# Two scan stages: the product with B made by TensorE for some state pairs, more C products on GpSimd

## The reference

```python
Bm, Cm = jnp.split(xs @ xp_w, 2, axis=-1)
dt = jax.nn.softplus(Bm @ dt_w + dt_b)
def step(hst, inp):
    xt, dtt, Bt, Ct = inp
    dA = jnp.exp(dtt[..., None] * A)
    hst = hst * dA + dtt[..., None] * Bt[:, None, :] * xt[..., None]
    yt = jnp.sum(hst * Ct[:, None, :], -1)
    return (hst, yt)
...
y = (y + D_skip * xs) * jax.nn.silu(gate)
```

## Time and profile before

| | us |
|---|---|
| median of 3 runs (5192.56 to 5204.24) | 5202.94 |
| the profiled execution, its time | 5190.3 |
| its span | 5188.7 |
| TensorE busy | 4065.8 (78%) |
| VectorE busy | 3570.5 (69%) |
| ScalarE busy | 2530.8 (49%) |
| GpSimd busy | 2856.4 (55%) |

### The profile page before, as it was taken

One profiled execution on the slowest core, in us unless ns is written; L12 is line 12 of the kernel. 1 busy time (PEld: TensorE's weight loads), 2 busy tenths in 40 slices (PEclk: granted clock), 3 DMA queues, 4 the chain that ended last, 5 costly groups with the idle time before them and its releaser, 6 DMA issues. The chain is left out here.

```text
span 5188.7 us, 47328 instructions
## 1 busy us (share of the span) xinstructions
PE 4065.8 (78%) x13734; PEld 1854.4 (36%) x13734; DVE 3570.5 (69%) x4968; ACT 2530.8 (49%) x3913; POOL 2856.4 (55%) x2181
## 2 busy tenths in 40 slices
PE   7999527982956988888887798997789777777776
PEld 2444203750423653333332444543333222222222
DVE  7998426121545759999998644444443699999999
ACT  5553311330445876666665244444346555555554
POOL 3776451027034439999996301113331489988997
PEclk8999759995977999999999899988889899999999
DMA  1100200211111115444443333321110343334443
GB/s 48 51 35 35 76 33 25 68 52 53 55 74 48 58 50 169 155 153 153 155 153 110 86 45 40 43 40 40 32 41 17 109 137 135 133 134 140 136 135 102
DMA packets 161701, 434.82 MB, mean 84 GB/s; under 512 B 28151, under 2 KB 51385, under 8 KB 160049
## 3 DMA queue, kind: packets, MB, share of 16 engines
...
## 5 line engine op out<-in xcount | busy, mean ns | idle before, releaser
L1680 ACT ACTIVATE mb_h<-m_dt,m_a_neg 128x512 f32<-128x512 f32 x1024 | 665.0, 681 | 725.8 <-DVE r L1835 332.9
L1539 PE MATMUL mb_y<-r,m_diag_y 128*128 128x512 f32 x1024 | 549.3, 671 | 273.0 <-POOL r L1760 164.6
L1826 DVE TENSOR_TENSOR_SCAN mb_h<-mb_h,m_u 128x1024 f32<-128x1024 f32 x320 | 733.9, 2294 | 10.8 <-DVE mb_h L1815 0.5
L1783 POOL TENSOR_TENSOR m_u<-m_bsb,m_xs 128x1024 f32<-128x1024 f32 x256 | 600.2, 2369 | 175.7 <-DMA m_bsb<-bc_rows 175.7
L1783 POOL TENSOR_TENSOR m_u<-m_bsb,m_dtx 128x1024 f32<-128x1024 f32 x256 | 596.0, 2359 | 50.9 <-DVE m_dtx L1867 28.2
L1539 PE MATMUL mb_y<-m_hc,w_common 128*128 128x512 f32 x1024 | 499.6, 628 | 149.5 <-DVE m_hc L1835 84.6
L1826 DVE TENSOR_TENSOR_SCAN m_hs<-mb_h,m_u 128x1024 f32<-128x1024 f32 x192 | 437.6, 2279 | 1.7 <-POOL m_u L1783 1.7
L1539 PEld LDWEIGHTS mb_y<-r,m_diag_y 128*128 128x128 f32 x1024 | 196.3, 207 | 621.0 <-POOL r L1760 245.3
L2309 DVE TENSOR_REDUCE at_mx<-at_ps_s 128x4 f32<-128x512 f32 (+1 forms) x256 | 243.2, 957 | 235.2 <-PE at_ps_s L2123 235.1
L1760 POOL TENSOR_TENSOR r<-m_hs,m_csb 128x1024 f32<-128x1024 f32 x128 | 308.2, 2408 | 118.0 <-DVE m_hs L1826 117.4
L1539 PEld LDWEIGHTS mb_y<-m_hc,w_common 128*128 128x128 f32 x1024 | 191.5, 197 | 449.2 <-issue 195.0
...
## 6 DMA issues: line engine op xcount, KB each, us to landing
m_bsb<-bc_rows SPq DMA_DIRECT2D x256, 512.0 KB, 4.9
m_csb<-bc_rows SPq DMA_DIRECT2D x256, 512.0 KB, 4.0
...
```

The costliest lines, as they stand in the source:

```text
L1539: mm = nc.tensor.matmul(ps_y[:, h], weight, hc[:, q % RING, s], start=False, stop=g == GROUPS - 1 and s == SG - 1)
L1680: ins = nc.scalar.activation(ps_h[:, q % 2, s], dt[:, i % 2, h], ACT.Exp, scale=a_neg[:, n:n + 1])
L1783: nc.gpsimd.tensor_tensor(u[:, q % RING], bsb[:, n % RING], dtx[:, i % 2, h].unsqueeze(1).broadcast_to([P, SG, TILE]), ALU.mult).then_inc( ...
L1826: V.tensor_tensor_scan(flat(to), flat(ps_h[:, q % 2]), flat(u[:, q % RING]), 0.0, ALU.mult, ALU.add).then_inc(h_ready, 1)
```

## The change

For some pairs (`by_pe`) the product with B is made by TensorE: pairs 4 to 7 of 8 in layer 2, all but pairs 0 and 4 in the last layer. A product u[d, t] = z[d, t] B[t] is a matmul of z, transposed to tokens by channels, with a diagonal matrix of B. Tokens are taken in four interleaved quarters k (t = 4r + k) and two rows j of 256, so a diagonal is 64 by 64.

- `turn_z` transposes z (dtx or x) of the next tile and `copy_z` (ScalarE) copies it to `zt`; `turn_b` and `copy_b` do so for B, into `bt`.
- `diagonals` (GpSimd) makes the diagonals of one pair into `dg` (2 slots) from a constant, `spots`, and `bt`.
- `make_u(q)` (TensorE) is 8 matmuls, 64 rows by 128 columns, rows 0 to 63 and 64 to 127 in turn, each into its own bank of `ps_h[:, q % 2]`. TensorE does it four units ahead in its order, before `sum_states(q - 4)`.
- For these units the decays go to SBUF, into the ring `u`, and the term lies in PSUM; the columns are ordered row, state, token, which `packed` and `spread` undo at the C product. Their B is not fetched, and `bsb` has 2 or 3 slots.
- C products: GpSimd takes all in the last layer and 9 of 16 in layer 2 (before 8 and 4), out of three `hs` slots.
- Silu, gate and project steps move by a unit or so, and take waits on `z_ready` and `z_in`.

The diff, cut to its core:

```diff
+    BR, HS = (3, 3) if l3 else (2, 3)
...
+        bsb = sb("bsb", [P, BR, SG, TILE])
...
+        hs = sb("hs", [P, HS, SG, TILE])
+        zt = sb("zt", [P, 2, 2, 4, P])
+        bt = sb("bt", [P, 2, 4, NSTATE])
+        dg = sb("dg", [P, 2, 4, SG, T // 4])
...
-        by_pool = [q % (2 if l3 else 4) == 0 for q in range(NU)]
+        by_pool = [True if l3 else q * 9 % 16 < 9 for q in range(NU)]
+        by_pe = [q % UNITS // 2 % 4 != 0 if l3 else q % UNITS // 2 >= 4 for q in range(NU)]
+        pe_units = [sum(by_pe[:q]) for q in range(NU + 1)]
+        fed_units = [q - pe_units[q] for q in range(NU + 1)]
+        z = xs if l3 else dtx
...
+        def slot_free(q, eng):
+
+            if q >= 2 and by_pool[q - 2]:
+                eng.wait_ge(h_ready, q - 1)
+            if q >= 2 and not by_pool[q - 2]:
+                eng.wait_ge(hc_ready, dve_units[q - 1])
...
                 elif a:
                     pe.wait_ge(sg_ready, 2 * a)
+                    pe.wait_ge(z_ready, 2 * a)
...
+                if h:
+                    pe.wait_ge(bt_ready, a + 1)
                 nc.tensor.matmul(ps_w[:, h], w["dt_w"][0:K, h * P:(h + 1) * P], low[0:K],
                                  start=True, stop=True).then_inc(dt_in, 1)
...
+            def turn_b(a):
+                pe.wait_ge(low_ready, a + 1)
+                rows_b = bcf[0:NSTATE].rearrange("p (r k) -> p k r", k=4)
+                for k in range(4):
+                    mm = nc.tensor.transpose(ps_w[:, 1, k * NSTATE:(k + 1) * NSTATE], rows_b[:, k],
+                                             w["eye"][0:NSTATE, 0:NSTATE])
+                mm.then_inc(bt_in, 1)
...
+                cols = z[:, a % 2, h].rearrange("p (r k) -> p k r", k=4)
+                for k in range(4):
+                    mm = nc.tensor.transpose(ps_w[:, bank, k * P:(k + 1) * P], cols[:, k], w["eye"])
+                mm.then_inc(z_in, 1)
+
+            def make_u(q):
+                i, g, h = place(q)
+                d = pe_units[q] // 2
+                pe.wait_ge(z_ready, 2 * i + 2)
+                pe.wait_ge(d_ready, d + 1)
+                slot_free(q, pe)
+                to = ps_h[:, q % 2].rearrange("p j (s r k) -> p j k s r", s=SG, k=4)
+                for k in range(4):
+                    for j in range(2):
+                        at = slice(j * 64, (j + 1) * 64)
+                        mm = nc.tensor.matmul(to[:, j, k], zt[at, i % 2, h, k], dg[at, d % 2, k], start=True, stop=True)
+                mm.then_inc(u_made, 1)
...
-                pe.wait_ge(dt_taken, 2 * min(i + 2, NT))
+                pe.wait_ge(dt_taken, 2 * min(i + 3, NT))
+                pe.wait_ge(z_ready, 2 * min(i + 2, NT))
...
+            turn_b(0)
             step_size(0, 0)
             step_size(0, 1)
+            turn_z(0, 0)
+            turn_z(0, 1)
+            for q in range(4):
+                if by_pe[q]:
+                    make_u(q)
...
-                    sum_states(i * UNITS + n)
+                    q = i * UNITS + n
+                    if q + 4 < NU and by_pe[q + 4]:
+                        make_u(q + 4)
+                    sum_states(q)
                     if n == (3 if l3 else 2) and more:
                         project(i + 1)
                     if n == (5 if l3 else 3) and more:
+                        turn_b(i + 1)
                         step_size(i + 1, 0)
                         step_size(i + 1, 1)
                     if n == (9 if l3 else 7) and i:
                         project_out(i - 1)
-                    if n == (11 if l3 else 10) and more:
+                    if n == 9 and l3 and more:
+                        turn_z(i + 1, 0)
+                    if n == 10 and l3 and more:
+                        gate(i + 1, 0)
+                        turn_z(i + 1, 1)
+                    if n == 12 and l3 and more:
+                        gate(i + 1, 1)
+                    if n == 10 and not l3 and more:
                         gate(i + 1, 0)
                         gate(i + 1, 1)
+                    if n == 14 and not l3 and more:
+                        turn_z(i + 1, 0)
+                        turn_z(i + 1, 1)
             project_out(NT - 1)
...
+            def copy_b(a):
+                act.wait_ge(bt_in, a + 1)
+                if a >= 2:
+                    act.wait_ge(d_ready, pe_units[(a - 1) * UNITS] // 2)
+                nc.scalar.copy(bt[:, a % 2].rearrange("p k n -> p (k n)"), ps_w[:, 1, 0:4 * NSTATE]).then_inc(bt_ready, 1)
+
+            def copy_z(a, h):
+                act.wait_ge(z_in, 2 * a + h + 1)
+                if a >= 2:
+                    act.wait_ge(u_made, pe_units[(a - 1) * UNITS])
+                nc.scalar.copy(zt[:, a % 2, h].rearrange("p k d -> p (k d)"), ps_w[:, 1 if l3 else h]).then_inc(z_ready, 1)
...
-                if n == (4 if l3 else 3):
+                if n == 4:
...
                 if n == (8 if l3 else 6):
+                    copy_b(a)
                     step_parts(a, 0)
+                if n in (11, 13) and l3:
+                    copy_z(a, n // 13)
                 if n == (8 if l3 else 7):
...
-                if n == 14 and a:
+                if n == (15 if l3 else 13) and a:
...
+                if by_pe[q]:
+                    if q >= RING:
+                        act.wait_ge(h_ready, q - RING + 1)
+                    to, step = packed(u[:, q % RING], q), dt[:, i % 2, h].rearrange("p (j t) -> p j t", j=2)
+                else:
+                    slot_free(q, act)
+                    to, step = ps_h[:, q % 2].unsqueeze(1), dt[:, i % 2, h].unsqueeze(1)
                 if q == 1:
                     act.wait_ge(sg_ready, 2)
                 for s in range(SG):
                     n = h * NSTATE + g * SG + s
-                    ins = nc.scalar.activation(ps_h[:, q % 2, s], dt[:, i % 2, h], ACT.Exp, scale=a_neg[:, n:n + 1])
+                    ins = nc.scalar.activation(to[:, :, s], step, ACT.Exp, scale=a_neg[:, n:n + 1])
                 ins.then_inc(da_ready, 1)
...
+                if not l3 and q >= UNITS and q % UNITS == 3:
+                    copy_z(q // UNITS, 0)
+                    copy_z(q // UNITS, 1)
...
+                    k = fed_units[2 * n] // 2
+                    if not by_pe[2 * n]:
+                        if k >= BR:
+                            sync.wait_ge(u_ready, (k - BR + 1) * 2)
+                        src = bc_d[i % 2, g * SG:(g + 1) * SG].rearrange("s t -> (s t)").unsqueeze(0).broadcast_to([P, SG * TILE])
+                        sync.dma_start(bsb[:, k % BR].rearrange("p s t -> p (s t)"), src).then_inc(b_in[k % BR], 16)
+                    if n >= RING:
                         free = (n - RING + 1) * 2
-                        if n >= RING and dst is bsb:
...
+                        if dve_units[free]:
                             sync.wait_ge(hc_ready, dve_units[free])
-                            if pool_units[free]:
-                                sync.wait_ge(hp_ready, pool_units[free])
-                        src = bc_d[i % 2, at:at + SG].rearrange("s t -> (s t)").unsqueeze(0).broadcast_to([P, SG * TILE])
-                        sync.dma_start(dst[:, s].rearrange("p s t -> p (s t)"), src).then_inc(done[s], 16)
+                        sync.wait_ge(hp_ready, pool_units[free])
...
+                nc.gpsimd.tensor_tensor(spread(hc[:, q % RING], q), packed(hs[:, k % HS], q), spread(csb[:, n % RING], q),
+                                        ALU.mult).then_inc(hp_ready, 1)
...
+                i, g, h = place(q)
+                d = pe_units[q] // 2
+                pool.wait_ge(bt_ready, i + 1)
+                if d >= 2:
+                    pool.wait_ge(u_made, 2 * (d - 1))
+                nc.gpsimd.tensor_tensor(dg[:, d % 2], w["spots"].unsqueeze(1).unsqueeze(1).broadcast_to([P, 4, SG, T // 4]),
+                                        bt[:, i % 2, :, g * SG:(g + 1) * SG].unsqueeze(3).broadcast_to([P, 4, SG, T // 4]),
+                                        ALU.mult).then_inc(d_ready, 1)
...
+                k = fed_units[q] // 2
+                if not by_pe[q]:
+                    pool.wait_ge(b_in[k % BR], (k // BR + 1) * 16)
+                    if q >= RING:
+                        pool.wait_ge(h_ready, q - RING + 1)
+                    nc.gpsimd.tensor_tensor(u[:, q % RING], bsb[:, k % BR],
+                                            dtx[:, i % 2, h].unsqueeze(1).broadcast_to([P, SG, TILE]), ALU.mult).then_inc(u_ready, 1)
+                if q + 4 < NU and by_pe[q + 4] and q % 2 == 0:
+                    diagonals(q + 4)
                 if q >= 3 and by_pool[q - 3]:
                     times_c(q - 3)
-                if q % UNITS == UNITS - 1 and i + 1 < NT:
...
+                if by_pe[q]:
+                    dve.wait_ge(u_made, pe_units[q + 1])
+                else:
+                    dve.wait_ge(u_ready, fed_units[q + 1])
...
```

(38 more changed lines are left out.)

56 lines of the change are left out of this document (37 added, 19 removed).

## The result

The changed kernel takes 5912.68 us (5899.93 to 5919.80), the kernel before 5197.75 us beside it: ratio 1.138, 95% interval 1.1342 to 1.1417. The forecast was 5690, the range 5420 to 5900. So the direction held, the size did not: 489 us of growth were predicted, 715 came.

What follows compares the result with a forecast made beforehand. VectorE was taken to bound both scan stages, GpSimd close behind. Inner tiles add 14 x (17.6 + 15.4) = 462 us; with first tiles, last tiles and lead-in 489; 5190 + 489 = 5679, forecast 5690, range 5420 to 5900.

Steps and rivals of the forecast that it cites:

- the loads: Scan stages: VectorE 59.3 and 48.2 us a tile; by loads alone a tile would be 60.6 and 53.3.
- rival 1: Both scan stages: loads decide, stalls overlap the work of others; 142 us saved, 5061; chance 0.10.
- make_u at 1.1: TensorE: 8 matmuls in overlapping row groups, 8 x 0.112 + 0.2 = 1.1 us each.
- The diagonals were booked at 1.28: GpSimd: 512-column diagonals take 1.28 us; short broadcast runs could make them up to 2.4.
- The places of the stalls: Inner tiles: VectorE waits at listed places, sum 26.3 us in the last layer and 22.0 in the second.
- The clock: TensorE, both stages: granted 0.97 and 0.94, so nearly all at 2.4 GHz; a lower clock kept for the upper end.
- the second layer's conv: Second layer: conv waits for z_ready, given by copy_z after decay(3), and delays decay(5); stall 3.6 us.
- the 0.6 us of copy_low: Last layer, after scan 5: make_u(7), sum(3), projections, copy_low and decay(7) hold up VectorE; stall 4.8 us.
- Edges: First tiles plus 10 (last layer) and 5 (second); last tiles plus 4 and 0; lead-in plus 4 each.
- (d) in the second layer: After C product 12: make_u(14), sum(10), gate, table loads, silus, decay(14) take 9.2 against 2.35; stall 6.9 us.
- The range: Whole kernel: 5420 with half of the stalls hidden, to 5900 with a slow make_u and a lower clock.
- rival 3: TensorE: make_u takes 2.0 us, giving 5790; at 3.9 TensorE is the bound and it passes 5900; chance 0.13.

Runs made afterwards that it cites:

- Experiment 6: The changed kernel, but TensorE makes no product with B (those stay on GpSimd) and the decays stay in PSUM: 5521.7 us, ratio 1.060.
- experiment 9: The kernel before, with zero-weight matmuls in TensorE's two longest idle stretches of a last-layer tile: 5199.2 us against 5195.4, ratio 1.0004.
- experiment 5: The changed kernel, with zero-weight matmuls only in TensorE's idle stretches, each group shorter than its stretch: 5751.3 us, ratio 1.105.

## Why the prediction came out short

Point by point, by its own steps:

- **What bounds it, and the loads**: right. In the kernel after VectorE is busy 927.5 us in the last stage, 58.0 a tile (booked 59.3), and 46.9 a tile in the second layer's (booked 48.2). Experiment 6 shows GpSimd's at 80.0 and 63.9 (booked 81.3 and 64.3, for that mix). That loads would not decide was right as well; rival 1 (5061) is out.
- **make_u at 1.1**: right. At the full rate the next instruction starts 1.09 us after it (4834.25 to 4835.34). The diagonals were booked at 1.28 and took 1.05; short runs did not lengthen them, they are faster.
- **The places of the stalls**: right, all ten. With TensorE at full rate their sum is 27.8 in the last layer (booked 26.3; the 0.5 and 0.3 of two small ones are in it) and 23.8 in the second (22.0).
- **The clock: this is the step that failed.** The prediction took the granted clock of the kernel before, 0.97 and 0.94, booked every make_u and every sum of its chains at 2.4 GHz, and kept a lower clock as a margin above, without a price. But in the kernel before TensorE is slow beside a busy VectorE, where it costs nothing (experiment 9); in the kernel after it is slow at the head of the chains. Its slow stretches follow from the stalls that the prediction had listed itself: in the last layer each of its three long waits for a scan (3.18, 5.58 and 6.32 us) is followed by a make_u of 2.08 instead of 1.16 and, in the rows above, a sum of 3.15 to 3.70 instead of 1.98. In the last layer the filled stretches took 8.5 us off each tile (95.6 to 87.1), in the second 3.3 (75.1 to 71.8): 14 x 11.8 = 165 us, where the kernel gained 161 as a whole.
- **The account of the difference.** Predicted 489, measured 715, so 226 are missing. (It is 223 against 5690, since the forecast stood on 5203 for the kernel before and was rounded.) Over the 14 periods between the first and the fifteenth gate product, the second layer grew by 284 us (booked 216) and the last by 386 (booked 246): 208 of the 226. The filled idle stretches give back 46 and 120 of them (experiment 5): 166 are the clock. Some 25 are the second layer's conv, in part at half rate (1.8 x 14), read from its row and not tested. The other 17 are the 0.6 us of copy_low (9) and other small terms.
- **Edges**: the other 20 us or so. From the end of the stage ahead to its first gate product the last layer took 33 us more than before, where 14 were booked, and the last tile of the second layer 8, where 0 was booked. What made them so was not tested.
- **(d) in the second layer** had 1.3 us too much: ScalarE's table load for silu_gate ran before the wait for the gate matmul, not behind it. It is 6.32 at full rate against 6.9, so 0.7 was missing elsewhere in it.
- **The range.** Its upper end came from rival 3, a slow make_u. The rival did not occur. A slow clock was named beside it and given no price. By the sizes measured since (8.5 us a tile in the last layer, 3.3 and the conv's 1.8 in the second) the price is 14 x 13.6 = 190, and 5880, an estimate in hindsight, would have been the middle instead of the edge.

By the Trainium skill (SBUF — State Buffer, the note on cachelines) a non-contiguous pattern in PSUM slows matmuls markedly, which spoke for rival 3. The trace disagrees: make_u writes every fourth word of PSUM, and its 16 instructions in two row groups take 1.09 us up to the next instruction, which is 8 x 0.112 by the contiguous ones of the earlier trace rows and the 0.2 of entry and exit.

The Trainium skill's page TensorE: Matmul & The Clock Gate (HAM oscillation — how this bites in real kernels) tells of a matmul kernel that waits in each step of its loop and starts each step at the lower clock. The rows of 4913.99, 4941.57 and 4960.93 agree: three waits of TensorE, three slow starts in a tile.
